# Last relational layer of a graph network: one-hot comparisons with the column as a broadcast second tensor

## The chip, the cores and the metric

The kernel runs on one core of a Trainium2 chip. The metric is the device time of one execution in microseconds; the kernel before is given by the median of three runs. The engines are TensorE (PE, matrix products; PEld is its weight load), VectorE (DVE), ScalarE (ACT), GpSimd (POOL) and SyncE (SP). Here POOL mostly issues indirect DMAs (gathers), and SP issues direct ones.

## The reference

Four graph layers over 6250 nodes of 64 features and 206250 edges (sorted by target) follow one another, each with a layer norm and a relu ahead of it and a residual sum behind it. The change is in the last:

```python
def _L3_gnn_ref(x, edge_index, edge_type, W_rel, W_self, b_self):
    out = x @ W_self.T + b_self
    src = x[edge_index[0]]
    msg = jnp.zeros((src.shape[0], W_rel.shape[1]), dtype=x.dtype)
    for r in range(W_rel.shape[0]):
        msg = msg + jnp.where((edge_type == r)[:, None], src @ W_rel[r].T, 0.0)
    out = out.at[edge_index[1]].add(msg)
    return jax.nn.relu(out)

h = jnp.maximum(_layernorm(x, axis=-1), 0.0)
x = x + _L3_gnn_ref(h, edge_index, edge_type_3, L3_gnn_W_rel, L3_gnn_W_self, L3_gnn_b_self)
```

For every edge the row of its source node, multiplied by the matrix of its relation, is summed into the target node.

## The kernel before, in words

Edges lie in [128 partitions x T columns], each partition holding a run of consecutive edges. The last layer goes through the columns in 2 x LP = 62 halves of HALF = 26 columns; `count(i, h)` numbers them, and each of the two buffers serves every second half. Of the 26 columns of a half, NGA = 21 are gathered: POOL issues one indirect DMA a column (L2975), which fetches 128 rows of the table of already multiplied rows, `y3_d`. Before a half it waits only for its indices (`s_idx`), which ACT stages two halves ahead.

The other ND = 5 columns are made "densely" without a gather. SP loads the codes of their edges, repeated over all partitions, into `rowb[h]` ([128 x 640], fp32; `load_ahead`, which waits for the one-hots of the half that used the buffer). DVE compares them with seven columns of node numbers, `col[:, k]`, and writes seven one-hot matrices `hot[h][:, k, :]` in bf16 (`onehots`, L3091). TensorE multiplies these by `parts3`, the node rows split into three bf16 parts: 21 matmuls of 128 x 448 for each of the five tiles (`tile`, L3196, into two PSUM banks in turn). DVE then masks and sums the product (`select`, L3099 and L3104), TensorE turns the rows (`turn_rows`, L3206), DVE copies them (`turned_rows`, L3111), TensorE multiplies by the three relation matrices (`relate`, L3216), and DVE picks the relation (`relation`, L3119 and L3127). The result goes into the same row buffer `g[h]` as the gathered rows.

When the 21 gathers have landed and the five dense columns are done, ACT copies the rows of the half by feature into PSUM (L2946, L2947) and the flags for equal targets into `keep` (L2948). DVE makes the running sums in one scan (L3134, `keep` in SBUF and `turned` in PSUM), ACT copies them back (L2955) and SP stores them. After the last half POOL gathers the segment ends (L3255), and the output is formed.

DVE's order is written out by hand in `turn`. In a half it is: scan of the half two before, select 0, relation and copy of the half before, one-hots 0 and 1 of the next half, select 1, relation, one-hots 2 and 3, select 2, copy, one-hots 4 and 5, select 3, relation, one-hot 6, select 4, copy. The prediction calls the three couples "pair 1" to "pair 3", and one-hot 6 "the single". Ahead of the loop DVE makes the digits, splits `hs` into the parts (L3066, L3070), compares seven one-hots in a row, and makes the masks (L3074, L3077). In the last pass it also does `link_and_bias` (L3082, L3083).

Of the kernel before, what the change touches and what calls it, by code (L numbers as in the profile page):

```python
# [14 lines left out]
ALU = mybir.AluOpType  # L15
ACT = mybir.ActivationFunctionType
X = mybir.AxisListType.X
P = 128
# [128 lines left out]
def build(nc, x, src, dst, edge_attr, edge_type, w0a, b0a, w0b, b0b, w1, b1, watt, att_s, att_d, batt, wf1, bf1, wf2,  # L147
# [57 lines left out]
    with top:  # L205
        def sb(name, shape, dt=f32, ctx=top):
            return ctx.enter_context(nc.sbuf_tensor(name, shape, dt))
# [32 lines left out]
        def bc(ap, shape):  # L240
            return ap.to_broadcast(shape)
# [2620 lines left out]
        with ExitStack() as ctx:  # L2862
            ND = 5
# [18 lines left out]
            rowb = [sb(f"dense_code_rows{h}", [P, ND * P], f32, ctx) for h in range(2)]  # L2882
            hot = [sb(f"dense_onehot{h}", [P, NJ, ND * P], bf16, ctx) for h in range(2)]
            col = sb("dense_columns", [P, NJ], f32, ctx)
# [24 lines left out]
            def count(i, h):  # L2909
                return i * 2 + h  # L2910
# [24 lines left out]
            with nc.Block() as block:  # L2935
# [85 lines left out]
                def _(e):  # L3021
# [63 lines left out]
                    def onehots(i, h, lo, hi):  # L3085
                        if lo == 0:
                            e.wait_ge(s_code_row[h], i * 16 + 16)
                            if not isinstance(i, int) or i:
                                e.wait_ge(s_tile, (count(i, h) - 1) * ND)
                        for k in range(lo, hi):  # L3090
                            e.tensor_scalar(hot[h][:, k, :], rowb[h][:, :], col[:, k:k + 1], None, ALU.is_equal)\  # L3091
                             .then_inc(s_hot, 1)

                    def select(i, h, m):
# [44 lines left out]
                    def turn(e, i, h):  # L3139
                        last, here, then = before(i, h), real(i, h), before(i, h, -1)  # L3140
                        if real(*before(i, h, 2)):
                            scan(*before(i, h, 2))
                        if here:
                            select(i, h, 0)
                        if real(*last):
                            relation(*last, 1)
                            turned_rows(*last, 2)
                        if here:
                            if real(*then):
                                onehots(*then, 0, 2)  # L3150
                            select(i, h, 1)
                        if real(*last):
                            relation(*last, 2)
                        if here:
                            if real(*then):
                                onehots(*then, 2, 4)
                            select(i, h, 2)
                            turned_rows(i, h, 0)
                            if real(*then):
                                onehots(*then, 4, 6)  # L3160
                            select(i, h, 3)
                            relation(i, h, 0)
                            if real(*then):
                                onehots(*then, 6, NJ)
                            select(i, h, 4)
                            turned_rows(i, h, 1)
                        if isinstance(i, int) and i == LP - 1 and h == 0:
                            link_and_bias()
# [160 lines left out]
```

## Time and profile before

| | |
|---|---|
| median of three runs | 7652.59 us (7649.28 to 7654.1) |
| span of the profiled execution (first to last instruction) | 7643.3 us |
| PE / DVE / POOL / ACT busy | 82% / 84% / 71% / 54% of the span |
| the stage of the change | about 5838 to 7560 us |
| mean granted TensorE clock over the span | 0.834 of full speed |

The profile is of one execution. The file of times gives the runs only as such, so the profiled execution's own time is known by its span; the median is 9.3 us above it. Views used: costs by line and shape within a stretch; waits (who waited for whom); busy time by stretch; and the timeline, whose rows have the start in us, the duration, the engine, the line, the operation, output and inputs, the number of instructions merged into the row, and in brackets the idle time of the engine before it with what ended it. "issue" is idle time in which an engine waited for nothing that the profile shows.

### The profile page before, as it was taken

The page shows a single profiled execution, that of the slowest core. Times are in us where ns is not written, and L with a number is a line of the kernel's source. Part 1 is how long each engine was busy: PE and PEld are TensorE (multiplying, and loading weights), DVE is VectorE, ACT ScalarE, POOL GpSimd, SP SyncE. Part 2 cuts the span into 40 slices and gives each one's busy share as a digit, 9 for nine tenths or more (in the row PEclk, how much of TensorE's full clock was granted, in tenths as well). Part 3 has the DMA queues.
Part 4 walks back from the last instruction along what each step waited for, and adds up shares of the span by engine and source line. Part 5 has one row for each costly group of instructions (what it writes and reads, how often), then busy time and mean ns, then how long its engine had stood idle before and what let it go on. Part 6 is the DMA issues. An engine that isn't in the chain of part 4 may idle for free. (4 is left out here: it accounts for less than half of the span.)

```text
span 7643.3 us, 144735 instructions
## 1 busy us (share of the span) xinstructions
PE 6305.5 (82%) x38830; PEld 4392.3 (57%) x38831; DVE 6452.2 (84%) x17467; ACT 4145.4 (54%) x10359; POOL 5414.8 (71%) x4893
## 2 busy tenths in 40 slices
PE   5988888888868999966777777777778999999994
PEld 3555544555437888855666666666674544444442
DVE  6999999999969999958999999999986766666664
ACT  4787778777836777734555555555522333333331
POOL 4888888888855565557777777777324777777776
PEclk9999999999978999955666666666656999999996
DMA  4444444444431111123433343343231222222222
GB/s 128 75 71 71 73 75 71 70 74 75 68 77 31 24 24 24 24 60 56 66 64 64 65 65 64 64 64 64 50 96 48 70 68 68 68 68 68 68 68 54
DMA packets 626463, 487.11 MB, mean 64 GB/s; under 512 B 513291, under 2 KB 530032, under 8 KB 616346
## 3 DMA queue, kind: packets, MB, share of 16 engines
q0 software_dynamic: 281600, 185.95, 20.9%
q1 hardware_dynamic: 342457, 293.43, 13.0%
q10 hardware_dynamic: 2304, 6.55, 0.2%
q8 instruction: 41, 0.67, 0.0%
q14 instruction: 61, 0.50, 0.0%
HBM read 303.43 MB, written 182.13 MB: 64 GB/s over the span
## 5 line engine op out<-in xcount | busy, mean ns | idle before, releaser
L973 POOL DMA_INDIRECT acc<-val,idx x1116 | 1722.2, 1543 | 397.9 <-issue 318.5
L2124 POOL DMA_INDIRECT tile_rows<-att_row_table,src_by_tile x1620 | 1529.4, 944 | 509.2 <-issue 490.3
L746 PE MATMUL banks<-part 128*128 128x490 bf16 (+1 forms) x7440 | 1569.1, 366 | 219.3 <-DVE part L828 219.2
L2975 POOL DMA_INDIRECT rows_l<-relation_table,idx x1302 | 1317.1, 1012 | 414.4 <-issue 396.4
L3196 PE MATMUL banks<-h_parts,dense_onehot 128*128 128x448 bf16 x6510 | 1355.2, 366 | 16.5 <-DVE dense_onehot L3091 16.5
L2245 PE MATMUL banks<-tile_rows,prob 128*128 x4032 | 855.0, 380 | 537.2 <-DVE kept_l L2343 536.1
L746 PEld LDWEIGHTS banks<-part 128*128 128x128 bf16 x7440 | 693.7, 97 | 997.4 <-DVE part L828 281.7
L2245 PEld LDWEIGHTS banks<-tile_rows,prob 128*128 128x128 f32 x4032 | 770.0, 285 | 635.8 <-issue 635.8
L3196 PEld LDWEIGHTS banks<-h_parts,dense_onehot 128*128 128x128 bf16 x6510 | 631.3, 101 | 673.8 <-issue 155.7
L904 ACT ACTIVATE digit_distance<-iota_row,dst_digits_negated 128x128 bf16<-128x128 f32 (+1 forms) x3224 | 868.7, 357 | 2.1 <-ACT dst_digits_negated L893 0.2
L1285 POOL DMA_INDIRECT gathered_rows<-h_table,gathered_index x600 | 577.9, 963 | 401.7 <-DMA gathered_rows<-h_table,gathered_index 239.0
L1339 DVE TENSOR_SCALAR hot_code<-columns_bf,codes 128x196 bf16<-128x196 bf16 x2400 | 687.0, 291 | 0.0
L828 DVE SCALAR_TENSOR_TENSOR part<-banks,src_digits,part 128x490 bf16<-128x490 f32 x992 | 671.9, 720 | 0.0
L1441 ACT CAST counts<-banks 128x784 bf16<-128x784 f32 x650 | 526.9, 819 | 244.5 <-PE banks L1490 240.3
L1338 DVE TENSOR_SCALAR hot_src_lo<-columns_bf,codes 128x128 bf16<-128x128 bf16 x2400 | 649.7, 274 | 3.2 <-ACT codes L1402 3.2
L2343 DVE SCALAR_TENSOR_TENSOR kept_l<-kept_l,fade,banks 128x65 f32<-128x65 f32 x2016 | 566.3, 281 | 59.4 <-PE banks L2245 5.3
L1515 PE MATMUL banks<-counts,h_parts 128*128 128x208 bf16 x4900 | 588.9, 264 | 0.0
L2172 ACT ACTIVATE edge_logit<-banks 128x1024 f32<-128x1024 f32 x252 | 257.8, 1023 | 586.6 <-DVE banks L2294 586.6
L2946 ACT COPY banks<-sums_by_feature 128x64 f32<-128x64 f32 x62 | 17.9, 289 | 922.7 <-DMA rows_l<-relation_table,idx 851.9
L3099 DVE TENSOR_TENSOR h_nodes<-banks,dense_mask_j 128x448 f32<-128x448 f32 x310 | 191.2, 617 | 372.2 <-PE banks L3196 369.7
L2253 PE MATMUL banks<-ident,run 128*128 128x128 f32 x2016 | 481.7, 418 | 4.6 <-ACT fade L2180 4.6
L1515 PEld LDWEIGHTS banks<-counts,h_parts 128*128 128x128 bf16 x4900 | 470.5, 98 | 9.7
(447 smaller groups left out, 11528.4 us busy)
## 6 DMA issues: line engine op xcount, KB each, us to landing
src_rows<-src_by_column SPq DMA_DIRECT2D x63, 1152.0 KB, 5.8
piece_sums<-kept_l SPq DMA_DIRECT2D x252, 264.0 KB
running_sums<-run SPq DMA_DIRECT2D x62, 832.0 KB, 4.0
attr<-in_edge_attr SPq DMA_DIRECT2D x61, 624.0 KB, 3.8
tile_rows<-att_row_table,src_by_tile POOLq DMA_INDIRECT x1620
rows_l<-relation_table,idx POOLq DMA_INDIRECT x1302
dense_code_rows<-src_by_column SPq DMA_DIRECT2D x62, 320.0 KB
acc<-val,idx POOLq DMA_INDIRECT x1116, 3.2
```

The lines of the kernel that those rows point to most:

```text
L746: last = e.matmul(ps[a][:, 0:ZW[a]], place0[(h * NZ + m) % 2][:, a, :], spread0[(h * NZ + m) % 2][n].rearrange("p b f -> p (b f)")[:, 0:ZW ...
L828: last = e.scalar_tensor_tensor(spread0[b][n], bc(ps[7][:, 0:ZB].unsqueeze(2), [P, ZB, W0]), dig[h][:, m, ZA:ZA + 1], bc(t.unsqueeze(1), [ ...
L904: last = e.activation(gap[n][:, r - a, :], iota[:, 0:w], ACT.Square, bias=away[n][:, r:r + 1])
L973: e.indirect_dma_start(acc_d[k], bass.IndirectOffsetOnAxis(ap=idx[h][:, r:r + 1], axis=0), val[h][:, r, :], None, compute_op=ALU.add).then ...
L1285: e.indirect_dma_start(grow[s][:, u, :], None, h1_d, bass.IndirectOffsetOnAxis(ap=gidx[s][:, u:u + 1], axis=0))\
L1338: e.tensor_scalar(hlo[slot(q)][:, u, :], cols[:, 0:P], code[s][:, 0, n:n + 1], None, ALU.is_equal)
L1339: last = e.tensor_scalar(hcd[slot(q)][:, u, :], cols[:, :], code[s][:, 1, n:n + 1], None, ALU.is_equal)
L1515: last = e.matmul(ps[4 + 1 - s][:, 0:BN * HT], parts4[:, m // 2, m % 2 * 2 * D:(m % 2 + 1) * 2 * D], table[1 - s][:, :, m // 2 * BN:(m // ...
L2124: e.indirect_dma_start(to, None, hx_d, bass.IndirectOffsetOnAxis(ap=src_col[:, t:t + 1], axis=0))\
L2245: last = e.matmul(summed(r), prob[u % 2][:, r, :], flat[:, bass.ds(cols[r], W1)], start=True, stop=True)
L2975: e.indirect_dma_start(g[h][:, r, :], None, y3_d, bass.IndirectOffsetOnAxis(ap=idx[h][:, r:r + 1], axis=0))\
L3196: last = e.matmul(ps[4 + b][:, 0:WJ], hot[h][:, k, m * P:(m + 1) * P], parts3[:, n, k * WJ:(k + 1) * WJ], start=(k == 0 and n == 0), stop= ...
```

## The change

The comparison of `onehots` stays a comparison for equality of the same values, with the same output. Its second operand is no longer given as a scalar for each partition (`tensor_scalar` with `col[:, k:k+1]`) but as a second input tensor (`tensor_tensor`), the same column repeated along the row by a zero step. `bc(ap, shape)` is `ap.to_broadcast(shape)`. Both inputs are fp32 in SBUF, the output is bf16 in SBUF. Order, waits and semaphores stay as they are. The line is issued 7 times for each of 62 halves.

```diff
                         for k in range(lo, hi):
-                            e.tensor_scalar(hot[h][:, k, :], rowb[h][:, :], col[:, k:k + 1], None, ALU.is_equal)\
+                            e.tensor_tensor(hot[h][:, k, :], rowb[h][:, :], bc(col[:, k:k + 1], [P, ND * P]), ALU.is_equal)\
                              .then_inc(s_hot, 1)
```

## Rows read from the trace of the kernel before

**Rows 1.** Costs by line, 5838 to 7560 us: shapes, count, busy us, mean ns, idle.
```profile
L2975 POOL DMA_INDIRECT rows_l<-relation_table,idx x1302 | 1317.1, 1012 | 414.4 <-issue 396.4 <-ACT idx L2939 17.9
...
L3091 DVE TENSOR_SCALAR dense_onehot<-dense_code_rows,dense_columns 128x640 bf16<-128x640 f32 x434 | 220.1, 542 | 0.0
...
L3070 DVE TENSOR_TENSOR h_nodes<-h_nodes,h_parts 128x3136 f32<-128x3136 f32 x2 | 6.9, 3426 | 0.1
...
L3074 DVE TENSOR_TENSOR dense_mask_j<-iota_row,dense_digits 128x2170 f32<-128x2170 f32 x1 | 2.4, 2406 | 0.0
...
L3077 DVE TENSOR_TENSOR dense_mask_r<-iota_row,dense_digits 128x930 f32<-128x930 f32 x1 | 1.1, 1115 | 0.0
```

**Rows 2.** View of line L2975: count, minimum, median and maximum in ns.
```profile
L2975 POOL DMA_INDIRECT rows_l<-relation_table,idx x1302: 940/944/4986, 5841.4 to 7554.1; - x186
```

**Rows 3.** Busy time of L2975's gathers by stretch: us, busy (instructions), clock, DMA.
```profile
5868.00:6075.60 207.60, 159.94 (x156) 1.00 0.26 66
...
6075.60:7468.60 1393.00, 1066.63 (x1072) 0.94 0.26 68
```

**Rows 4.** Waits, 5840 to 7643 us: who waited for whom, us, times, longest.
```profile
ACT banks L2946 <- DMA rows_l<-relation_table,idx: 851.9, 57, 18.9
...
POOL rows_l L2975 <- issue: 396.4, 1301, 0.3
...
DVE h_nodes L3099 <- PE banks L3196: 369.7, 197, 4.7
```

**Rows 5.** Timeline, 6519 to 6547 us: start, duration, engine, line, instructions merged, idle.
```profile
6519.11 3.75 DVE L3134 TENSOR_TENSOR_SCAN sums_by_feature<-same_by_feature,banks 128x1728 f32<-128x1728 f32 x1 [4.18 <-ACT same_by_feature L2948]
...
6525.43 1.36 POOL L2975 DMA_INDIRECT rows_l<-relation_table,idx  x1 [0.30 <-issue]
...
6525.67 1.00 DVE L3091 TENSOR_SCALAR dense_onehot<-dense_code_rows,dense_columns 128x640 bf16<-128x640 f32 x2
...
6528.74 1.00 DVE L3091 TENSOR_SCALAR dense_onehot<-dense_code_rows,dense_columns 128x640 bf16<-128x640 f32 x2
...
6533.68 0.62 DVE L3099 TENSOR_TENSOR h_nodes<-banks,dense_mask_j 128x448 f32<-128x448 f32 x1 [3.93 <-PE banks L3196]
...
6535.59 1.00 DVE L3091 TENSOR_SCALAR dense_onehot<-dense_code_rows,dense_columns 128x640 bf16<-128x640 f32 x2
...
6540.93 0.55 DVE L3091 TENSOR_SCALAR dense_onehot<-dense_code_rows,dense_columns 128x640 bf16<-128x640 f32 x1
...
6546.44 3.75 DVE L3134 TENSOR_TENSOR_SCAN sums_by_feature<-same_by_feature,banks 128x1728 f32<-128x1728 f32 x1 [1.16 <-ACT same_by_feature L2948]
...
6546.45 0.94 POOL L2975 DMA_INDIRECT rows_l<-relation_table,idx  x1 [0.30 <-issue]
```

**Rows 6.** Timeline, 6553 to 6566 us, VectorE.
```profile
6553.03 0.99 DVE L3091 TENSOR_SCALAR dense_onehot<-dense_code_rows,dense_columns 128x640 bf16<-128x640 f32 x2
...
6556.10 1.00 DVE L3091 TENSOR_SCALAR dense_onehot<-dense_code_rows,dense_columns 128x640 bf16<-128x640 f32 x2
...
6558.04 0.62 DVE L3099 TENSOR_TENSOR h_nodes<-banks,dense_mask_j 128x448 f32<-128x448 f32 x1 [0.93 <-PE banks L3196]
...
6559.96 1.00 DVE L3091 TENSOR_SCALAR dense_onehot<-dense_code_rows,dense_columns 128x640 bf16<-128x640 f32 x2
...
6565.37 0.55 DVE L3091 TENSOR_SCALAR dense_onehot<-dense_code_rows,dense_columns 128x640 bf16<-128x640 f32 x1
```

**Rows 7.** Timeline, 7500 to 7506 us: a tensor_tensor and a gather.
```profile
7500.84 3.41 DVE L3083 TENSOR_TENSOR own<-own,b 128x3136 f32<-128x3136 f32 x1
...
7501.35 3.73 POOL L2975 DMA_INDIRECT rows_l<-relation_table,idx  x1 [0.30 <-issue]
```

**Rows 8.** Timeline, 5571 to 5576 us, another stage: two tensor_tensor and a gather.
```profile
5571.30 2.29 DVE L2495 TENSOR_TENSOR self_message<-block_rows,self_weight 98x2048 f32<-98x2048 f32 x1
...
5571.68 2.73 POOL L2458 DMA_INDIRECT block_sums<-piece_sums,last_piece_rows  x1 [12.54 <-DVE scaled L2490]
...
5573.69 2.29 DVE L2500 TENSOR_TENSOR scaled<-scaled,self_message 98x2048 f32<-98x2048 f32 x1
```

## The prediction

> **What bounds the kernel now.** I began with the engine totals of the page. VectorE (DVE) is busy 84% and GpSimd (POOL) 71%, over a span of many stages with different limits, so the totals decide nothing. The change touches one stage, the last relational layer, which runs from 5838 to 7560 us. There I read the costs by line [rows 1]. The one-hot comparisons, L3091, are 434 instructions of 542 ns. The gathers of L2975 are 1302 DMA issues, 21 for each of 62 halves (a half is one value of count(i, h)). They take 1317.1 us with a mean of 1012 ns, although the view of that line gives a median of 944 and a longest of 4986 [rows 2].
>
> Next come the waits of the stage [rows 4]. POOL never waits for work: 1301 of its 1302 gaps are "issue", 396.4 us, or 0.30 each. ACT waits 851.9 us for the gathers' data. DVE waits 369.7 us for TensorE before L3099, 197 times, on average 1.88. So the gathers set the pace. ACT transposes what they bring, the scan of L3134 waits for ACT, and DVE and TensorE fit in between. A half costs 21 x (0.94 + 0.30), or 26.1 us, plus whatever lengthens gathers. The timeline [rows 5] shows the slack that DVE has: before the scan it stood idle 4.18 us for ACT in one half and 1.16 in the next, and halves of these two kinds alternate in the steady state.
>
> Then what lengthens gathers. In the steady stretch 1072 gathers take 1066.6 us [rows 3]. At the median of 0.944 each they would take 1012.0, so 54.6 us are excess, 1.07 for each of the 51 halves. In the stretch before it 156 gathers carry 159.9 - 147.3 = 12.7 us [rows 3]. The timeline shows who causes it. The gather of 6525.43 takes 1.36 beside the two one-hots of 6525.67, and ends 0.12 after them. The scan of 6546.44 lies over the gather of 6546.45, which takes 0.94: the scan reads one tensor in SBUF and one in PSUM, and costs POOL nothing. In the steady stretch only gathers that overlap L3091 exceed 0.96 in the timeline. So the change acts twice: on DVE, which has slack, and on the gathers, which have none.
>
> **The change part by part.** *The comparison itself.* 434 tensor_scalar of 0.542 go [rows 1] and 434 tensor_tensor come, with 640 elements a row, fp32 in and bf16 out. No instruction of before has this form, so I take it from the slope of its neighbours [rows 1]. L3077 (930 elements, broadcast operands) takes 1115 ns and L3074 (2170) takes 2406. The slope is 1291 / 1240 = 1.041 ns an element, and 640 elements give 1115 - 290 x 1.041 = 813 ns. L3070, dense, takes 3426 ns for 3136; at the same slope 640 give 827. I take 0.82, bounds 0.81 to 0.83. A zero step in the operand costs nothing in L3074 and L3077, which have it. That is 0.28 us more each, 434 x 0.28 = 121 us of DVE, 1.95 a half. Two in a row start 0.08 before the other's end now (2 x 0.54 against 1.00), so a pair grows from 1.00 to 1.56.
>
> *Where these 1.95 go.* DVE's order in a half is scan, select 0, relation, pair 1, select 1, relation, pair 2, select 2, pair 3, select 3, relation, one single, select 4, scan. Pair 1 delays select 1 by 0.56 and pair 2 moves with it. TensorE is then still in the tile whose bank select 0 has already freed, so it isn't held. Pair 2 ends 1.12 later than now. In the half of 6533.68 the wait behind it was 3.93 and swallows it; in the other it was 0.93 at 6558.04 [rows 5, 6], so select 2 starts 0.1 to 0.2 late. Pair 3 and the single lie ahead of select 3 and select 4, which wait 1.88 on average for TensorE [rows 4] against a growth of 0.56 and 0.28. The scan is reached at most 0.2 later, against idle time of 1.16 and 4.18. Price on the path: zero. If this cover were gone altogether, the half with 1.16 would exceed it by 0.8, which averages 0.4 a half. The SP queue's load of the next code rows waits for the last one-hot and is issued 0.3 later with most of a half in hand: zero. TensorE's first tile of the next half waits for the single, which ended more than 6 us before it: zero.
>
> *The gathers.* This decides. What does a tensor_tensor with both inputs in SBUF do to a gather? The rows of own + b [rows 7] show it. L3083 runs from 7500.84 to 7504.25, and the gather that starts at 7501.35 inside it takes 3.73 and ends at 7505.08, which is 0.83 after it. In another stage L2495 runs from 5571.30 to 5573.59, and the gather of 5571.68 ends at 5574.41, 0.82 after it [rows 8]. L2500 starts at 5573.69, while that gather is running, and doesn't hold it. So such an instruction holds a gather only if the gather *starts* inside it. The gather then ends 0.82 after it, and a second such instruction later in the gather's course costs nothing. A tensor_scalar also holds a gather near its end: the 1.36 above ended 0.12 after a one-hot [rows 5]. The new form is thus longer by half, but catches a gather at one point instead of two.
>
> The Trainium skill, in "SBUF — State Buffer", section "Who interferes with whom", says that a tensor_tensor with both inputs in SBUF contends with GpSimd's reads, and adds that a probe found tensor_tensor not to stall a DMA, descriptor generation needing the write side (inferred). The rows side with the first half of this: the gather of 3.73 was held [rows 7]. By the second half alone it would be the first rival below.
>
> Now I walk through two steady halves [rows 5, 6] with one-hots of 0.82, gathers of 0.94 and gaps of 0.30. Pair 1 occupies 6525.67 to 6527.23. The gather of 6525.43 starts before it and is free; the next starts at 6526.67, inside the second one-hot, and ends at 6528.05: 0.44 lost. Pair 2 is now at 6529.30 to 6530.86. The gather of 6529.59 falls into its first one-hot and ends at 6530.94: 0.41. Pair 3 stays at 6535.59: the gather of 6536.22 starts 0.19 before its first one-hot ends: 0.07. The single, 6540.93 to 6541.75, catches the gather of 6541.27: 0.36. Sum 1.28. In the second half pair 1 (6553.03) catches the gather of 6554.08 (0.39), pair 2 (now 6556.66) that of 6556.96 (0.40), pair 3 (now 6560.07) that of 6561.09 (0.42), and the single at 6565.37 none, since one gather starts 0.13 before it and the next at 6566.49 after it. Sum 1.21.
>
> The mean is 1.25 against 1.07 now: +0.18 x 51 = +9 us. In the stretch before, 156 gathers are 7.4 halves, with 12.7 / 7.4 = 1.71 each now: 7.4 x (1.25 - 1.71) = -3 us. The opening and the closing halves, with their seven one-hots in a row, I put at 0, with bounds of -1 and +2. **The sum is +6 us.** If phases were random instead, a one-hot of 0.82 would catch a gather's start over 0.70 of 1.25 us and cost 0.35 on average, so 0.20 x 7 = 1.4 a half: +17 - 2 = +15.
>
> The span of the profiled execution is 7643.3 us; the median of the timed runs, 7652.6, is 9.3 more, and what lies around the span is not touched. Forecast: 7652.6 + 6 = 7659 us.
>
> **The rivals.**
> *One: tensor_tensor doesn't hold gathers.* The excess of L3091 falls away: 54.6 + 12.7 = 67 us, 7585 us. DVE and TensorE could follow, having 1.16 and 4.18 idle against 1.1 to be won. For it: the L2500 and the scan that come over running gathers cost nothing [rows 5, 8]. Against it: both gathers that start inside such an instruction were held to its end [rows 7, 8]. Chance 8%.
> *Two, on the slower side: a near miss turns into a hit.* My walk passes two narrow places. The gather of 6536.22 asks 0.19 before the first one-hot of pair 3 ends. If it asks more than some 0.1 later, the second one takes it to 6537.15 + 0.82 instead: +0.74. The gather of 6565.24 starts 0.13 before the single. If it starts 0.15 later it ends 0.82 after the single's end at 6566.19: +0.83. Each recurs every second half, so one costs 0.4 x 51 = +20 us, 7679, and both cost 7699. The durations above are good to 0.01, but the sum of a half's gaps and shifts is hardly good to 0.1. Chance 30%, nearly all on one of the two.
> *Three: the DVE and TensorE loop becomes the bound.* It takes DVE being late for the scan by 0.8 in the shorter half, 0.4 x 51 = +20 on top, 7679. Against it stand 1.88 of mean wait in front of L3099. Chance 4%.
> That the form isn't slower on DVE at all (some faster way through a broadcast operand) speaks against L3074 and L3077, and leaves the time about where it is.
>
> **How the numbers follow.** Forecast 58%, own range 7650 to 7668; rival one 8%, two 30%, three 4%. 0.2% is 15 us, about what a measurement of this kernel can tell from no change. Faster holds rival one and a lucky phase: 9%. Slower is rivals two and three: 33%. Same: 58%. The range of 8 in 10 leaves out rival one and the double hit. It goes from 7645 (phases 0.25 a half better than walked) to 7692 (one hit and random phases elsewhere).
>
> **What the profile after would show.** L3091 as TENSOR_TENSOR x434 at 0.81 to 0.83; 0.27 or 0.54 would fell the first step. POOL's idle time still all "issue" in the loop, and ACT L2946 waiting for DMA: the gathers still pace. The steady mean of a gather at 0.944 + 1.25 / 21 = 1.00 us, against 0.995 now; 0.95 would be rival one, 1.02 or more rival two. Gathers lengthened by one-hots ending 0.82 after one, none 0.12 after one. DVE's idle time before the scan still present, 0 to 4 us; if it were nil in steady halves, with POOL still unhindered, rival three. A half at 27.4 us between scans, against 27.2 to 27.4 now.

## The result, and the profile after

The changed kernel takes 7700.97 us (median of 4 runs, 7698.54 to 7703.4) against 7650.93 (4 runs, 7648.17 to 7654.1) for the kernel before on the same chip: a ratio of 1.0066, 95% interval 1.0054 to 1.0078. It is 50 us slower, where 7659 was forecast and 7645 to 7692 was the range. The span of its profiled execution is 7696.7 us, 53.4 more than before.

The costs by line of the changed kernel, 5838 to 7660 us, answer to [rows 1] (busy us, mean ns, then idle time and what ended it):

```profile
L2975 POOL DMA_INDIRECT rows_l<-relation_table,idx x1302 | 1368.7, 1051 | 414.4 <-issue 396.4 <-ACT idx L2939 17.9
...
L3091 DVE TENSOR_TENSOR dense_onehot<-dense_code_rows,dense_columns 128x640 bf16<-128x640 f32 x434 | 337.7, 812 | 0.0
```

The comparisons cost VectorE 117.6 us more, as forecast. The gathers cost POOL 1368.7 - 1317.1 = 51.6 us more with the same 396.4 us of issue gaps. That is 51.6 of the 53.4 us of the span, so the loss sits on POOL, inside the gathers. The waits of the changed kernel say who paces whom (us in total, times, longest); they answer to [rows 4]:

```profile
ACT banks L2946 <- DMA rows_l<-relation_table,idx: 919.5, 58, 20.6
POOL rows_l L2975 <- issue: 396.4, 1301, 0.3
...
DVE h_nodes L3099 <- PE banks L3196: 244.7, 170, 5.1
DVE sums_by_feature L3134 <- ACT same_by_feature L2948: 221.2, 56, 19.4
```

VectorE still waits, for TensorE (it absorbs 125 us of the longer comparisons there) and for ACT; ACT waits longer for the gathers. The gathers by stretch in the changed kernel answer to [rows 3] (start and end, length, busy (instructions), clock, DMA share, GB/s). The middle stretch is the steady one again:

```profile
5868.00:6088.20 220.20, 172.37 (x158) 0.98 0.26 64
6088.20:7521.20 1433.00, 1106.63 (x1072) 0.95 0.26 67
```

The steady excess over 0.944 a gather is 1106.6 - 1012.0 = 94.6 us against 54.6, so 40 of the 51.6 us arise here: 1.86 a half instead of 1.07, and a half of 28.1 us on average instead of 27.3. The stretch before it carries 172.4 - 149.2 = 23.2 instead of 12.7: 10.5 us more, where the prediction had 3 less.

Two halves in the timeline of the changed kernel, 6526 to 6560 us, show the forms of hold; they answer to [rows 5, 6] (start, duration, engine, line, [idle before]):

```profile
6526.73 1.55 DVE L3091 TENSOR_TENSOR dense_onehot<-dense_code_rows,dense_columns 128x640 bf16<-128x640 f32 x2
6527.04 1.32 POOL L2975 DMA_INDIRECT rows_l<-relation_table,idx  x1 [0.30 <-issue]
...
6531.75 1.54 DVE L3091 TENSOR_TENSOR dense_onehot<-dense_code_rows,dense_columns 128x640 bf16<-128x640 f32 x2
6532.42 1.70 POOL L2975 DMA_INDIRECT rows_l<-relation_table,idx  x1 [0.30 <-issue]
...
6544.31 3.75 DVE L3134 TENSOR_TENSOR_SCAN sums_by_feature<-same_by_feature,banks 128x1728 f32<-128x1728 f32 x1 [2.91 <-ACT same_by_feature L2948]
6544.41 0.94 POOL L2975 DMA_INDIRECT rows_l<-relation_table,idx  x1 [0.30 <-issue]
...
6557.52 0.40 DVE L3111 COPY h_nodes<-banks 64x256 f32<-64x256 f32 x1
6557.66 2.56 POOL L2975 DMA_INDIRECT rows_l<-relation_table,idx  x1 [0.30 <-issue]
6557.85 1.54 DVE L3091 TENSOR_TENSOR dense_onehot<-dense_code_rows,dense_columns 128x640 bf16<-128x640 f32 x2
```

- 6527.04, a *simple hold*, at pair 2: the gather starts inside the first one-hot, which ends at 6527.54, and ends 0.82 after that. The second one-hot, from 6527.47, costs nothing. This is the prediction's rule. Ahead of pair 2 stands a reduction of 0.37 us (L3127).
- 6532.42, a *hold to the end of the pair*, at pair 3, ahead of which stands the copy of L3111: this gather, too, starts inside the first one-hot, 0.14 before it ends (6532.56). It isn't let go there, but kept to the end of the second (6533.29) + 0.83.
- 6557.66, a *led hold*: the gather starts before either one-hot, 0.19 ahead of the first, inside the copy. By the prediction's rule it is free. It is kept through both one-hots and ends 0.83 after the second (6559.39), 1.6 us late.

I put each gather above 0.96 us to the pair that its record overlaps. In the 51 steady halves pair 1 costs 0.42 a half, pair 2 0.39, pair 3 1.07 and the single 0.00. All 51 gathers at pair 2 are let go at the end of the first one-hot. At pair 3 none is: 22 start 0.12 to 0.23 ahead of it (led, 1.5 to 1.6 us each), and 29 start 0.67 to 0.94 after it begins (0.5 to 0.8 us each), 13 of these before the second one-hot does; every one ends 0.82 after the second. Pair 1 also stands behind a copy (0.27 us, of the half before). It is led twice; its other gathers start inside its second one-hot.

### The profile page after: what moved, and what is told of

Read it like the earlier page. It is cut to its first block and busy times, and to the rows that moved or that the text cites. A ratio compares the mean times of both kernels' runs of the same rounds, so it can differ in the third digit from the quotient of the medians.

```text
span 7696.7 us, 144735 instructions
## 1 busy us (share of the span) xinstructions
PE 6296.6 (82%) x38830; PEld 4388.8 (57%) x38831; DVE 6566.0 (85%) x17467; ACT 4145.8 (54%) x10359; POOL 5465.7 (71%) x4893
## 5 line engine op out<-in xcount | busy, mean ns | idle before, releaser
L2975 POOL DMA_INDIRECT rows_l<-relation_table,idx x1302 | 1368.7, 1051 | 414.4 <-issue 396.4
L825 DVE TENSOR_TENSOR part<-banks,src_digits 128x640 bf16<-128x640 f32 x496 | 406.5, 820 | 64.5 <-PE banks L746 62.4
```

Of the source, the lines that this page charges most:

```text
L2975: e.indirect_dma_start(g[h][:, r, :], None, y3_d, bass.IndirectOffsetOnAxis(ap=idx[h][:, r:r + 1], axis=0))\
```

## The experiments

The theory after the result: (1) the time follows the held gathers and nothing else, VectorE's added work being covered; (2) most of the 50 us are lost at pair 3, by where it falls and by the copy ahead of it. The rivals: VectorE's own time ahead of the later pairs is paid for, or the form of the comparison alone sets the price of each pair.

**ts_one_port: a comparison as slow as the new one, but through one port.** The comparison stays a `tensor_scalar`. Its output rows are padded, so that the engine takes one element a step.

```diff
-            hot = [sb(f"dense_onehot{h}", [P, NJ, ND * P], bf16, ctx) for h in range(2)]
+            hot = [sb(f"dense_onehot{h}", [P, NJ, ND, P + 2], bf16, ctx) for h in range(2)]
...
-                            e.tensor_scalar(hot[h][:, k, :], rowb[h][:, :], col[:, k:k + 1], None, ALU.is_equal)\
+                            e.tensor_scalar(hot[h][:, k, :, 0:P], rowb[h][:, :].rearrange("p (m c) -> p m c", c=P),
+                                            col[:, k:k + 1], None, ALU.is_equal)\
```

> The comparison of before (tensor_scalar, one SBUF input), but the one-hots are written in rows of 128 with a gap of 2, so that input and output have different outermost counts (640 and 5). I expect that DVE then takes one element a step, as long as in the changed kernel: L3091 about 0.81 us. Theory A (what costs time is that the comparison holds gathers, through its second SBUF input or its two-element form): with neither, gathers beside one-hots take 0.944, the steady excess of 1.07 us a half goes, only what other instructions of the opening and closing hold (some 11 us) stays, about 7580 us. Theory B (the longer comparison on DVE costs the 50 us): about 7700 us. If L3091 stays at 0.54 the run says nothing on B and the gathers stay held: about 7651 us.

Measured: 7581.92 us, ratio 0.9907 (0.9891 to 0.9924). The view of the comparison's line in this kernel (minimum, median, maximum in ns) and its gathers in the costs by line, 5838 to 7660 us:

```profile
L3091 DVE TENSOR_SCALAR dense_onehot<-dense_code_rows,dense_columns x434: 857/864/875, 5864.1 to 7430.9; 128x640 bf16<-128x640 f32 x145
```

```profile
L2975 POOL DMA_INDIRECT rows_l<-relation_table,idx x1302 | 1248.0, 959 | 415.9 <-issue 395.3 <-ACT idx L2939 20.6
```

The comparisons are slower than in the changed kernel (0.864 against 0.810), and the kernel is 119 us faster than it and 68 faster than before. In the timeline a pair behind the copy lets a gather pass, whether it starts inside the first one-hot or inside the copy itself (this kernel, 6534 and 7418 us):

```profile
6534.77 1.65 DVE L3091 TENSOR_SCALAR dense_onehot<-dense_code_rows,dense_columns 128x640 bf16<-128x640 f32 x2
6534.80 0.94 POOL L2975 DMA_INDIRECT rows_l<-relation_table,idx  x1 [0.30 <-issue]
...
7418.62 0.27 DVE L3112 COPY h_nodes<-banks 64x128 f32<-64x128 f32 x1
7418.74 0.94 POOL L2975 DMA_INDIRECT rows_l<-relation_table,idx  x1 [0.30 <-issue]
7418.82 1.65 DVE L3091 TENSOR_SCALAR dense_onehot<-dense_code_rows,dense_columns 128x640 bf16<-128x640 f32 x2
```

So the duration of the comparison isn't what costs; its form is. The Trainium skill, in "VectorE: DVE Perf Modes", section "Mode 2×_2P — use both read ports for one tensor", asks for an outermost dimension that is even, or equal for source and destination. Here a source of 640 in one run and an output of 5 x 128 leave that mode (5 is odd), and the 0.864 against 0.542 agrees. The copy, whose input is in PSUM, holds nothing by itself: the gather of 7418.74 starts 0.12 into it and 0.08 ahead of the pair, and takes 0.94.

**f16_one_port: the same with 16-bit codes**, so that the comparison is short as well.

```diff
+    codes_d = dram("dense_codes_f16", [(T + HALF) * P], mybir.dt.float16)
...
-            rowb = [sb(f"dense_code_rows{h}", [P, ND * P], f32, ctx) for h in range(2)]
+            rowb = [sb(f"dense_code_rows{h}", [P, ND * P], mybir.dt.float16, ctx) for h in range(2)]
```

> As ts_one_port (gaps in the output rows), and the code rows in 16-bit floats (codes below 896 are exact), so all elements have two bytes. Expected: L3091 at about 0.54 us through one side only, if DVE takes two 16-bit elements a step. Theory A: gathers beside one-hots at 0.944, about 7580 us, as ts_one_port, since DVE's time is not on the path. Theory B: as before, 7651 us. If the 16-bit rows open the form with both sides, L3091 falls below 0.4 and gathers are held a little: some 7610 us.

Measured: 7579.69 us, ratio 0.9905 (0.9889 to 0.9922), comparisons of 0.531 us, gathers 1247.0 us in all. 0.33 us less in each of 434 comparisons, 145 us of VectorE, are worth 2 us, which is within the scatter. This and ts_one_port beat both kernels.

**one_port_delay_b: ts_one_port with a memset ahead of pair 3**, in every half (it ran as 150 words, 0.18 us).

```diff
+            idle = sb("idle_time", [P, 300], bf16, ctx)
...
                             turned_rows(i, h, 0)
+                            e.memset(idle[:, :], 0.0)
```

> The one-element-a-step tensor_scalar of ts_one_port with a memset of 300 numbers ahead of the third pair in every half. If DVE's own time costs nothing and only the holding of gathers does: 7582 us, as without the memset, and gathers of 0.944 us in all steady halves. If time added to DVE ahead of the third pair is what the stage pays for: some 7610 to 7680 us.

Measured: 7581.01 us, ratio 0.9915 (0.9899 to 0.9932), gathers 1247.1 us. The memset costs nothing where nothing is held.

**tt_pair3 and tt_rest: one part of the change alone.** In tt_pair3 only pair 3 is a `tensor_tensor`; in tt_rest all but pair 3.

```diff
+                            if lo == 4:
+                                e.tensor_tensor(hot[h][:, k, :], rowb[h][:, :], bc(col[:, k:k + 1], [P, ND * P]), ALU.is_equal)\
+                                 .then_inc(s_hot, 1)
+                            else:
+                                e.tensor_scalar(hot[h][:, k, :], rowb[h][:, :], col[:, k:k + 1], None, ALU.is_equal)\
+                                 .then_inc(s_hot, 1)
```

> tensor_tensor for pair 3 alone (one-hots 4 and 5), tensor_scalar for the other five. Theory A (holds, the worst being a pair right behind the copy of L3111, which keeps a gather for both its instructions): pair 3's hold rises from 0.57 to some 1.1 us a half, the others' stays at 0.52, so +27 in the steady stretch and some more in the opening: 7680 us (7670 to 7690). Theory B (DVE time, 2 of 7 one-hots): +14, 7665 us.

> tensor_tensor for pairs 1 and 2 and the single, tensor_scalar for pair 3. Theory A: pair 1 stays at 0.41 us of hold a half, pair 2 rises from 0.12 to 0.39, pair 3 stays near 0.6 (0.4 to 1.0, its place moves): +14 steady and some 5 in the opening, 7670 us (7660 to 7685). Theory B (5 of 7 one-hots): +36, 7687 us.

Measured: tt_pair3 7653.98 us, ratio 1.0004 (0.9994 to 1.0014); tt_rest 7703.12, ratio 1.0066 (1.0049 to 1.0083). Both theories missed. The new form at the pair that pays most costs nothing; the new form everywhere else costs the whole loss, and pair 3, still the old form, then holds gathers for 0.86 a half against 0.57 before. The price belongs to the places where pairs fall among the gathers, and pairs 1 and 2 move them. In the 51 steady halves of tt_rest pair 1 is led 10 times, where the changed kernel has 2, and costs 0.65 a half instead of 0.42. Its timeline shows such a led hold at pair 1, and a hold of the old form at pair 3 (its lines are shifted: L3115 is the copy):

```profile
6526.39 0.27 DVE L3115 COPY h_nodes<-banks 64x128 f32<-64x128 f32 x1
6526.45 2.50 POOL L2975 DMA_INDIRECT rows_l<-relation_table,idx  x1 [0.30 <-issue]
6526.58 1.54 DVE L3092 TENSOR_TENSOR dense_onehot<-dense_code_rows,dense_columns 128x640 bf16<-128x640 f32 x2
...
6535.87 1.61 POOL L2975 DMA_INDIRECT rows_l<-relation_table,idx  x1 [0.30 <-issue]
6536.03 0.41 DVE L3115 COPY h_nodes<-banks 64x256 f32<-64x256 f32 x1
6536.36 1.00 DVE L3095 TENSOR_SCALAR dense_onehot<-dense_code_rows,dense_columns 128x640 bf16<-128x640 f32 x2
```

The second gather starts ahead of copy and pair; the old form catches it near its end and lets it go 0.12 after (6537.36), as the gather of 6525.43 in the prediction.

**copy_behind: the changed kernel with the copy of L3111 moved behind pair 3.**

```diff
                             select(i, h, 2)
-                            turned_rows(i, h, 0)
                             if real(*then):
                                 onehots(*then, 4, 6)
+                            turned_rows(i, h, 0)
```

> The changed kernel with the copy of L3111 that stands ahead of pair 3 put behind it. In the changed kernel a pair 3 that starts 0.2 us after a gather, right behind that copy, keeps the gather for both of its instructions: 2.56 us, 21 times in the 51 steady halves. Theory P (the time hangs on where a pair falls against the gathers' starts): pair 3 comes 0.33 earlier, the gather starts inside its first one-hot and is let go at that one's end, so the hold falls from 1.6 to about 0.6 in those halves and from 0.75 to 0.4 in the others: about 29 us less, 7672 us. Theory C (a fixed price for each tensor_tensor, wherever it lies): as the changed kernel, 7701 us.

Measured: 7678.31 us (7671.46 to 7691.64), ratio 1.0037 (1.0022 to 1.0051). Its profiled run has a span of 7689.8 and is the longest of the five. No 1.6 us hold is left at pair 3, which costs 0.50 a half instead of 1.07; but the single now costs 0.28 and pair 1, still behind its copy and led 9 times, 0.58. Ahead of pair 3 now stands a reduction of 0.92 us, and all 31 steady gathers that start inside the first one-hot are let go at its end (this kernel's timeline, 6530 us: 6529.96 to 6530.77 is the first, and the gather ends at 6531.60; at 6363 us the first ends at 6364.10 and the gather at 6364.93):

```profile
6529.12 0.92 DVE L3104 TENSOR_REDUCE h_nodes<-h_nodes 128x64 f32<-128x448 f32 x1
6529.96 1.55 DVE L3091 TENSOR_TENSOR dense_onehot<-dense_code_rows,dense_columns 128x640 bf16<-128x640 f32 x2
6530.06 1.54 POOL L2975 DMA_INDIRECT rows_l<-relation_table,idx  x1 [0.30 <-issue]
6531.43 0.41 DVE L3111 COPY h_nodes<-banks 64x256 f32<-64x256 f32 x1
```

```profile
6363.29 1.55 DVE L3091 TENSOR_TENSOR dense_onehot<-dense_code_rows,dense_columns 128x640 bf16<-128x640 f32 x2
6363.96 0.97 POOL L2975 DMA_INDIRECT rows_l<-relation_table,idx  x1 [0.30 <-issue]
```

The gather of 6363.96 starts at the same place in its pair as that of 6532.42 in the changed kernel, 0.67 after the pair begins. Behind the copy it took 1.70, behind the reduction 0.97; another, 0.72 after the pair begins (7145 us), took 0.94. So what kept the gather of 6532.42 is the copy ahead of the pair, not the nearness of the second one-hot. By the medians 23 of the 50 us come back (in the profiled run, at the slow end, 14 us of gathers). So the copy ahead of pair 3 is a cause, and part of what is won there is lost again at pair 1 and the single.

**add_for_copy_b: the copy made as an addition of zeros.** Is it the copy's form?

```diff
-                        e.tensor_copy(hrow_t[k][:, 0:w * P], bank_t(k)[:, 0:w * P]).then_inc(s_htc, 1)
+                        e.tensor_tensor(hrow_t[k][:, 0:w * P], bank_t(k)[:, 0:w * P], bc(zcol[0:D, 0:1], [D, w * P]), ALU.add).then_inc(s_htc, 1)
```

> The changed kernel with the copy of the turned rows (L3111) made as a tensor_tensor add of the same rows and a tile of zeros. If it is the form of the copy that begins the long hold ahead of the third pair: gathers there of at most 1.7 us and some 7680 us. If any short instruction right ahead of the pair does: the 2.5 to 2.6 us gathers stay and the time is 7695 to 7710 us.

Measured: 7707.17 us (7696.6 to 7711.97), ratio 1.0082 (1.0065 to 1.0099), as the changed kernel. The led holds stay, 21 at pair 3 (this kernel's timeline; L3113 is the addition):

```profile
6528.13 0.40 DVE L3113 TENSOR_TENSOR h_nodes<-banks,zero_column 64x256 f32<-64x256 f32 x1
6528.46 1.54 DVE L3093 TENSOR_TENSOR dense_onehot<-dense_code_rows,dense_columns 128x640 bf16<-128x640 f32 x2
6528.62 2.22 POOL L2976 DMA_INDIRECT rows_l<-relation_table,idx  x1 [0.31 <-issue]
...
6554.17 0.41 DVE L3113 TENSOR_TENSOR h_nodes<-banks,zero_column 64x256 f32<-64x256 f32 x1
6554.31 2.55 POOL L2976 DMA_INDIRECT rows_l<-relation_table,idx  x1 [0.30 <-issue]
```

It is not the copy's form alone. The gather of 6528.62 even starts 0.09 after the addition, 0.16 into the first one-hot, and is still kept through both, while that of 6530.06 above, 0.10 into the first one-hot and behind a reduction, was not. Nor is it that the instruction ahead is short, as the expectation had it: the reduction ahead of pair 2 takes 0.37 us, less than this addition, and behind it all 51 gathers are let go at the first one-hot.

**after_delay and after_delay_100_b: the changed kernel with a memset between the copy and pair 3**, of 300 numbers (0.31 us) and of 100 (0.14 us).

```diff
+            idle = sb("idle_time", [P, 300], f32, ctx)
...
                             turned_rows(i, h, 0)
+                            e.memset(idle[:, :], 0.0)
                             if real(*then):
```

> The changed kernel with a memset of 300 elements (some 0.4 us of DVE) ahead of pair 3, so that more work is done on DVE. Theory P: pair 3 comes 0.35 later, the gather that was kept for 2.56 is free and the next is kept some 0.7, the others' hold falls by 0.3: about 25 us less than the changed kernel, 7675 us, although DVE does more. Theory C: 7701 us. If DVE's time counted: 7701 + 62 x 0.35, 7722 us.

> The changed kernel with a shorter memset (100 numbers) between the copy of the turned rows and the third pair. If the hold runs from the copy through whatever stands back to back behind it: 2.5 to 2.7 us gathers and 7710 to 7750 us, between the changed kernel (7701) and the one with 300 numbers (7747). If the place in the cycle alone decides: anything from 7680 to 7750, without an order by the memset's length.

Measured: after_delay 7747.01 us, ratio 1.0130 (1.0113 to 1.0147); after_delay_100_b 7723.21 (7714.7 to 7723.4), ratio 1.0101 (1.0084 to 1.0118). The first was expected to help and cost 46 us more: it doesn't part the hold, it adds to it (timeline of after_delay, 6573 us; the pair ends at 6575.42 and the gather 0.83 later):

```profile
6573.29 0.41 DVE L3112 COPY h_nodes<-banks 64x256 f32<-64x256 f32 x1
6573.43 2.82 POOL L2976 DMA_INDIRECT rows_l<-relation_table,idx  x1 [0.30 <-issue]
6573.71 0.31 DVE L3160 MEMSET idle_time<- 128x300 f32 x1
6573.94 1.48 DVE L3092 TENSOR_TENSOR dense_onehot<-dense_code_rows,dense_columns 128x640 bf16<-128x640 f32 x2
```

The loss grows with the memset's length, while VectorE stands idle longer before the scan (4.59 us on average in the steady halves against 3.68 in the changed kernel). In one_port_delay_b a memset costs nothing, so the 46 us are held gathers: 1414.3 - 1368.7 = 45.6. The longer hold behind the memset is only a part of them. In the steady halves of after_delay pair 3 costs 1.38 a half instead of 1.07; the single, 0.35 instead of nothing, and pair 1, 0.60 instead of 0.42, bring more than that together, since they too fall elsewhere among the gathers.

**before_delay: the same memset in the kernel before.**

> The kernel before with the same memset ahead of pair 3. Theory P: pair 3's hold of 0.57 a half changes with its place; by the positions in the trace one kind of half loses 0.2 less and the other 0.3 more: 7655 us, within 20 us either way. Theory C: 7651 us. If DVE's time counted: 7672 us.

Measured: 7652.88 us, ratio 1.0007 (0.9998 to 1.0017). The memset's 19 us of VectorE aren't paid for here either. The run doesn't part theory P from theory C.

**f16_tt_full: a tensor_tensor with both inputs in SBUF, but short.** Codes and columns are 16-bit, the columns written out to full rows.

```diff
-            col = sb("dense_columns", [P, NJ], f32, ctx)
+            col = sb("dense_columns", [P, NJ, ND * P], mybir.dt.float16, ctx)
...
+                            e.tensor_tensor(hot[h][:, k, :], rowb[h][:, :], col[:, k, :], ALU.is_equal)\
```

> Still a tensor_tensor with two SBUF inputs, but short: code rows and columns as 16-bit floats (exact here), the columns written out in full rows, so that DVE takes two elements a step; the masks are stored in 16 bits to make room. L3091's instruction about 0.5 us. Theory H (two SBUF inputs hold a gather only at its start, so the price goes with the length): some 0.6 us of hold a half in place of 1.88, 7615 us (7600 to 7640, places decide). If the form as such costs, whatever the length: 7700 us. If two-input instructions hold no gather when short: 7580 us.

Measured: 7619.34 us, ratio 0.9960 (0.9946 to 0.9974), comparisons of 0.478 us, gathers 1284.9 us. The form holds gathers here too, 0.60 a half in the steady stretch, in place of none with a longer one-port comparison (0.864). So for this form, unlike the one-port form, shorter seems better: 0.60 a half at 0.478 us, 1.88 at 0.81. The columns are full rows here and 16 bits wide, and no run parts that from the length.

Four more ran on a chip on which the kernel before itself took 9667 us; three of them were run again, as above. The fourth, after_delay_600, has a memset of 600 numbers in bf16, which takes 0.31 us, as that of after_delay. Against the kernel before on that chip one_port_delay took 1.0014, add_for_copy 0.9973, after_delay_100 0.9966 and after_delay_600 0.9744 of its time: another order than above. In these four traces GpSimd stands idle for 1009 to 1386 us ahead of the gathers, 414 in the changed kernel above, and VectorE hardly at all ahead of the scan (at most 0.03 us on average). The gathers don't set the pace there, so the prices of this document hold only where they do. What made that chip slow is not known. The forms of hold are the same: in these traces, too, gathers passed the one-port pairs untouched and were led by the addition and by the memsets.

**All of it in one table.** Spans are those of the profiled runs, the gathers' busy time that of the costs by line:

| kernel | span | gathers, us | span - gathers |
|---|---|---|---|
| one_port_delay_b | 7577.4 | 1247.1 | 6330.3 |
| f16_one_port | 7578.4 | 1247.0 | 6331.4 |
| ts_one_port | 7580.5 | 1248.0 | 6332.5 |
| f16_tt_full | 7617.6 | 1284.9 | 6332.7 |
| before_delay | 7641.6 | 1318.9 | 6322.7 |
| before | 7643.3 | 1317.1 | 6326.2 |
| tt_pair3 | 7649.6 | 1320.1 | 6329.5 |
| copy_behind | 7689.8 | 1354.9 | 6334.9 |
| add_for_copy_b | 7694.8 | 1375.1 | 6319.7 |
| after | 7696.7 | 1368.7 | 6328.0 |
| tt_rest | 7702.8 | 1372.0 | 6330.8 |
| after_delay_100_b | 7712.9 | 1384.9 | 6328.0 |
| after_delay | 7741.1 | 1414.3 | 6326.8 |

The span moves by 164 us and the last column by 15. Whatever was done to VectorE, the time is, to within 15 us, the time of the gathers plus a constant.

## Why the prediction was wrong

- *The gathers pace the stage and VectorE has slack*: right. POOL's gaps are the same 396.4 us, and the table shows the rest.
- *A comparison of 0.82, bounds 0.81 to 0.83*: right, 0.810 in the median and 0.812 in the mean, so the slope of neighbouring shapes served.
- *VectorE's 1.95 us a half are hidden*: right. VectorE stands idle before the scan for 3.68 us on average over the steady halves, against 2.62 before. The longer comparisons of ts_one_port, 2.26 us a half more than before, cost nothing.
- *"Such an instruction holds a gather only if the gather starts inside it"*, "and a second such instruction later in the gather's course costs nothing": this is the step that failed. Three instructions and two gathers had been read for it, [rows 7, 8], none of them with a copy directly ahead. Behind a copy the pair acts as one block, which begins up to 0.23 us ahead of it: a gather that starts in it ends 0.82 after the *second* one-hot. The prediction's order of VectorE left both copies out, so that pair 1 and pair 3, which stand behind one, looked like pair 2, which doesn't. The kernel before shows the block for the old form, in 25 of its 51 steady halves, and in the first half that the prediction walked. The gather at pair 3 is not among the rows that it shows:

```profile
6535.26 0.41 DVE L3111 COPY h_nodes<-banks 64x256 f32<-64x256 f32 x1
6535.59 1.00 DVE L3091 TENSOR_SCALAR dense_onehot<-dense_code_rows,dense_columns 128x640 bf16<-128x640 f32 x2
6535.95 1.47 POOL L2975 DMA_INDIRECT rows_l<-relation_table,idx  x1 [0.30 <-issue]
```

  It starts inside the first one-hot, which ends at 6536.13, and ends at 6537.42, 0.83 after the second. The led hold is there as well, at 6023 us, in the stretch of which I took the excess of 12.7 us without looking into it, and once in the steady stretch, at 6096:

```profile
6023.68 0.41 DVE L3111 COPY h_nodes<-banks 64x256 f32<-64x256 f32 x1
6023.81 2.02 POOL L2975 DMA_INDIRECT rows_l<-relation_table,idx  x1 [0.30 <-issue]
6024.01 1.00 DVE L3091 TENSOR_SCALAR dense_onehot<-dense_code_rows,dense_columns 128x640 bf16<-128x640 f32 x2
```

  That gather ends 0.82 after the pair, not 0.12 as the ones from which I drew the rule for the old form.
- *The walk of two halves, 1.25 a half*: pair 1 was given 0.42 and measured 0.42, pair 2 0.41 and 0.39. Pair 3 was given 0.25 and measured 1.07, the single 0.18 and 0.00. The term that was mis-sized is pair 3: the steady sum is 1.88 instead of 1.25, (1.88 - 1.25) x 51 = 32 us (1.86 by the sum over all gathers), and the opening halves, booked at -3, measured +10.5.
- *The places of the walk at pair 3 were good; only the price put on them was wrong.* In the first half the walk has a gather at 6536.22, 0.63 into pair 3. It priced it at 0.07; kept to the end of the pair, 6537.15 + 0.82, it costs 0.81. In the second half it has gathers at 6556.96, held to 6558.30, and so at 6558.60 and 6559.84, which is 0.23 ahead of pair 3 (6560.07) and inside the copy. It took that one for free; kept to 6561.63 + 0.82 it costs 1.67, in place of the 0.42 booked for the next. The mean is 1.24 for pair 3 where 0.25 was booked, and the forecast would have been about 7709 us (an estimate: 7659 + 0.99 x 51, shifts left out), near the 7701 measured.
- *Why the costly place comes so often.* In 19 of the 51 steady halves of the changed kernel TensorE's first tile behind the scan takes 4.15 us (in the one shown the granted clock is 1.00, the higher of the two levels). In all 19 pair 3 starts 7.0 us after pair 1, and a gather 0.19 to 0.20 ahead of pair 3. The kernel before has such a tile in every second half, too, but there pair 3 starts 6.9 us after pair 1 and the gather 0.38 to 0.41 ahead of it, too early for the block. In the two halves whose rows follow, pairs 1 and 2 hold gathers for 0.77 us instead of 0.61, and the gather ahead of pair 1 starts 0.1 closer to it; so the next ones come 0.2 later against pair 3. The rows of TensorE, of before in the second half that was walked and of the changed kernel in the half of the 2.56:

```profile
6553.75 4.14 PE L3196 MATMUL banks<-h_parts,dense_onehot 128*128 128x448 bf16 x21
```

```profile
6551.52 4.15 PE L3196 MATMUL banks<-h_parts,dense_onehot 128*128 128x448 bf16 x21
```

  In the other halves the tile takes longer, 6.79 us in the first half that was walked, at a mean granted clock of 0.60, between the two levels, and pair 3 comes later. The strict alternation of the two kinds is gone in the changed kernel: of its 50 spacings from scan to scan 26 are 27.5 to 27.8 us and 24 are 28.5 to 28.9, in no fixed order. What sets that order is open.
- *Rival two* (a near miss turns into a hit) has the right direction. That its double hit, 7699, is near the 7701 measured is luck. At its first place gathers were kept through both one-hots for the 0.7 to 0.8 us that it priced, but because of the copy ahead and not because they came late: copy_behind lets such a gather go. Its second place, the single, never turned; the led holds brought the rest. *Rival one* is refuted: with the holds really gone the time is 7582, near the 7585 that it named, and the changed kernel is 119 above it. *Rival three* is refuted by ts_one_port, the time of which leaves VectorE's loop room at 0.864 a comparison.
- *The range*: its upper end, 7692, stands for one hit and random phases elsewhere, both priced by the rule that failed; gathers held from ahead of a pair were not in it. tt_pair3 and tt_rest, where the parts of the change cost 4 and 53 us and neither theory named either, show that sums over places don't add when every hold moves the next.

## What to carry to other kernels

When GpSimd issues indirect DMAs back to back, look at what VectorE runs beside them: a comparison in the one-port form (output rows padded) cost nothing here even at 0.864 us, while the two-port form of 0.542 cost 68 us and one of 0.81 with two inputs in SBUF cost 119. That holds where the gathers set the pace. When the price depends on where short instructions fall among periodic ones, test the rule on every row of the stretch that it is to explain before anything is added up with it, and the *longest* rows first; look at what stands ahead of the instruction as well. Where every hold moves the next, give the sum a range of the worst place in each period, and don't walk it to a hundredth.

## What the runs showed of the hardware that I had not expected

- A tensor_tensor with both inputs in SBUF holds GpSimd's indirect DMA issue, and the issue ends 0.82 to 0.83 us after it. The Trainium skill, in "SBUF — State Buffer", section "Who interferes with whom", infers that this form should leave descriptor generation alone; the 1368.7 us of gathers against 1248.0 speak otherwise, and the measurement decides. The same section says that this form contends with GpSimd's reads, and the gather reads its indices, `idx`, from SBUF; whether it is this read that waits, no run shows.
- The same section of the Trainium skill says that against a VectorE instruction in a two-port mode whoever issues first has the shared ports for the whole instruction. No run here shows VectorE made to wait for a gather of 0.94 us: all comparisons lay over gathers, and they took 531 to 610 ns in the kernel before and 801 to 837 in the changed one.
- Behind a copy (0.27 or 0.41 us), an addition (0.40) or a memset (0.14 or 0.31) two back-to-back comparisons hold a gather as one block, up to 0.82 us behind the end of the second; a gather took up to 2.82 us. In the changed kernel the block reaches 0.23 us ahead of pair 3 and 0.14 ahead of pair 1. Behind a reduction, of 0.37 us (pair 2) or 0.92 (copy_behind), a gather that starts inside the first is let go at its end: 51 of 51 and 31 of 31 in the steady halves. A gather 0.67 into the pair took 1.70 behind the copy and 0.97 behind the reduction.
- So it isn't the shortness of the instruction ahead. The copy and the addition take their rows from PSUM and the memset reads nothing, while both reductions read SBUF; whether that is the difference is not tested. The copy and the memset hold nothing ahead of one-port comparisons.
